# Three cross attentions over 1,500 keys: more probabilities turned by VectorE, moves issued from two queues, router logits made transposed

## The reference, cut to what matters

```
keys   = values = rope(ctx)                      # 1500 x 64, the same in all three layers
scores = q @ keys.T                              # (56 tokens x 16 heads) x 1500
probs  = softmax(scores, axis=-1)
out    = (probs @ values) @ folded_output
```

```
dom    = softmax(gelu(mean_tokens(h) @ te_W1 + b1) @ te_W2 + b2) @ affinity.T    # one row per sequence
logits = h @ Wr.T + dom[sequence]                # 896 tokens x 64
```

## Time and profile before

| | us |
|---|---|
| median of 3 runs | 3226.8 (3226.05 to 3234.65) |
| profiled execution, its own time | 3225.33 |
| its span | 3223.5 |
| TensorE busy | 2964.8 (92%) |
| VectorE busy | 1783.4 (55%) |
| ScalarE busy | 1324.0 (41%) |
| POOL busy | 808.5 (25%) |

### The profile page before, as it was taken

The page is one execution under the profiler, slowest core; times in us unless marked ns, Lnnn a source line. Parts: engine busy times, 40 slices in busy tenths (PEclk is TensorE's granted clock), DMA queues, the critical chain, the costliest instruction groups (busy, mean ns, idle before and its releaser), DMA issues. The chain is left out here.

```text
span 3223.5 us, 49820 instructions
## 1 busy us (share of the span) xinstructions
PE 2964.8 (92%) x18697; PEld 1751.9 (54%) x18697; DVE 1783.4 (55%) x3608; ACT 1324.0 (41%) x2300; POOL 808.5 (25%) x743
## 2 busy tenths in 40 slices
PE   4889999978999989899999989989899999677999
PEld 3755555564455453355655657753355566446444
DVE  6567777723232257777775233347777775655222
ACT  4456666611111142466665122222466665424221
POOL 4324444400316024322232000004322332201000
PEclk8899999978999999999999999999999999888999
DMA  1245556412122202255654010012255564001111
GB/s 32 68 121 142 129 146 140 120 50 97 61 92 78 88 26 82 57 136 131 135 136 124 30 41 26 26 39 78 56 133 133 134 138 121 15 12 23 40 39 33
DMA packets 221451, 266.71 MB, mean 83 GB/s; under 512 B 127178, under 2 KB 148796, under 8 KB 218764
## 3 DMA queue, kind: packets, MB, share of 16 engines
q1 hardware_dynamic: 220348, 262.19, 31.5%
q10 hardware_dynamic: 864, 1.33, 0.1%
HBM read 120.92 MB, written 21.38 MB: 44 GB/s over the span
## 5 line engine op out<-in xcount | busy, mean ns | idle before, releaser
L1777 ACT ACTIVATE l2x_shared<-l2x_shared,l2x_a_low 128x1500 f32<-128x1500 f32 x112 | 173.2, 1546 | 140.8 <-DVE l2x_shared L1733 136.8
L1777 ACT ACTIVATE l1x_shared<-l1x_shared,l1x_a_low 128x1500 f32<-128x1500 f32 x112 | 173.3, 1547 | 138.9 <-DVE l1x_shared L1733 134.9
L1777 ACT ACTIVATE l0x_shared<-l0x_shared,l0x_a_low 128x1500 f32<-128x1500 f32 x112 | 173.4, 1548 | 125.0 <-DVE l0x_shared L1733 122.4
L1647 PE MATMUL l2x_a_S_ps<-l2x_kt,l2x_a_q 64*128 64x366 f32 (+1 forms) x896 | 171.9, 501 | 1.7 <-DMA l2x_a_q<-l2x_qa 1.1
L1647 PE MATMUL l0x_a_S_ps<-l0x_kt,l0x_a_q 64*128 64x366 f32 (+1 forms) x896 | 172.0, 501 | 0.5 <-DVE l0x_shared L1733 0.5
L1647 PE MATMUL l1x_a_S_ps<-l1x_kt,l1x_a_q 64*128 64x366 f32 (+1 forms) x896 | 172.0, 501 | 0.6 <-DVE l1x_shared L1733 0.6
L2016 DVE TENSOR_TENSOR l0f_times_up<-l0f_gate,l0f_U 128x448 f32<-128x448 f32 x64 | 39.8, 622 | 237.3 <-PE l0f_U L1934 237.3
L1985 ACT ACTIVATE l0f_gate<-l0f_G 128x448 f32<-128x448 f32 x72 | 39.2, 544 | 311.1 <-PE l0f_G L1929 311.1
L1733 DVE TENSOR_SCALAR_CACHE_REDUCE l0x_shared<-l0x_a_S_ps 128x768 f32<-128x768 f32 x112 | 107.3, 958 | 102.8 <-PE l0x_a_S_ps L1647 101.8
L1733 DVE TENSOR_SCALAR_CACHE_REDUCE l2x_shared<-l2x_a_S_ps 128x768 f32<-128x768 f32 x112 | 107.3, 958 | 85.2 <-PE l2x_a_S_ps L1647 83.3
L1733 DVE TENSOR_SCALAR_CACHE_REDUCE l1x_shared<-l1x_a_S_ps 128x768 f32<-128x768 f32 x112 | 107.3, 958 | 84.9 <-PE l1x_a_S_ps L1647 82.8
(11 more groups left out here) (667 smaller groups left out, 6623.7 us busy)
## 6 DMA issues: line engine op xcount, KB each, us to landing
l0x_space<-normed SPq DMA_DIRECT2D x192, 96.0 KB
l1x_space<-normed SPq DMA_DIRECT2D x192, 96.0 KB
l2x_space<-normed SPq DMA_DIRECT2D x192, 96.0 KB
l0x_space<-l0x_a_blocks SPq DMA_DIRECT2D x186, 72.0 KB, 2.5
l1x_space<-l1x_a_blocks SPq DMA_DIRECT2D x186, 72.0 KB, 2.3
l2x_space<-l2x_a_blocks SPq DMA_DIRECT2D x186, 72.0 KB, 2.6
l0f_gu<-in_L_ffn_gu SPq DMA_DIRECT2D x36, 256.0 KB, 2.6
l0x_a_q<-l0x_qa SPq DMA_DIRECT2D x32, 224.0 KB, 3.9
```

The costliest lines, as they stand in the source:

```text
L1647: last = pe.matmul(S_ps[:, 2 * pair + rows_, 0:w], q[lane, b % 2, k * 128:(k + 1) * 128], kt[lane, b % 2, pair * W1:pair * W1 + w], start= ...
L1777: act.activation(p[:, n % 2], p[:, n % 2], ACT.Exp, bias=low[:, n % 2, 1:2], scale=-1.0, accum_out=den[:, b % 2, k:k + 1]).then_inc(exp_re ...
```

## The change

Of the 1,500 keys, VectorE now turns 1,024 (NB = 8 slots of 128) and TensorE 476 (NP = 4 slots of 119).

- `turn` does four transposes of 119, into one half of T_ps (T_ps[n % 2]), and so waits for the copy of tile n - 2. `keep` is one copy of 512.
- `block_turn` turns 1,024 columns. Moved rows of group 0 are 4 KB instead of 3 KB, those of group 1 are 3 KB instead of 2.25 KB; POOL's own copies grow alike.
- `values`: slots 0 to 3 come from `pt`, 4 to 11 from the moved blocks. Group 0 is split 2, 2, 4, 4 over its tiles instead of 3, 3, 3, 3.
- `move`: SP issues the DMAs of two lanes (6 of 12) for each group; ScalarE's queue issues the other 6, at tiles 3 and 6, behind exp(n + 2).
- The reciprocals are taken once a batch.
- The columns of the scores are laid out anew, so that TensorE's and VectorE's parts are each in one piece; for it the turned keys of stage 0 are copied by four copies instead of two.
- The rope tables hold each value once, and POOL's three multiplications read them through a view that gives each value twice.
- Router: the token part of the logits is made transposed (64 experts x 512 tokens, two chunks each), the first half ahead of the small network, the second inside it; `dom` is added to both, ScalarE and VectorE copy one half each, and eight transposes bring them to lg_ps.

The diff, cut to its core:

```diff
-KD, KP, KJ = 128, 122, 6
+KD, KP, NB, NP = 128, 119, 8, 4
+NS = NB + NP
...
+        def times(out, src, table):
+            n = src.shape[2] // 2
+            return pool.tensor_tensor(out.rearrange("p s (f two) -> p s f two", two=2), src.rearrange("p s (f two) -> p s f two", two=2),
+                                      table.unsqueeze(3).to_broadcast([KD, NS, n, 2]), ALU.mult)
...
-    W1, W2, JB = 3 * KD, 3 * KP, KJ * 32
-    PIECES = {5: (0, 0, 3), 6: (0, 3, 6), 7: (0, 6, 9), 8: (0, 9, 12), 9: (1, 0, 4), 10: (1, 4, 8), 11: (1, 8, 12)}
+    W1, W2, JB = 3 * KD, KD + 2 * KP, NB * 32
+    PIECES = {5: (0, 0, 2), 6: (0, 2, 4), 7: (0, 4, 8), 8: (0, 8, 12), 9: (1, 0, 4), 10: (1, 4, 8), 11: (1, 8, 12)}
...
-                    move(sp, b, 0, range(4))
+                    move(sp, b, 0, range(2))
...
-                    move(sp, b, 1, range(4) if b + 1 < B else range(2))
+                    move(sp, b, 1, range(2))
...
-                    if ctx is not None and n % T == 5 and n // T + 1 < B:
-                        pe.wait_ge(k_kept, 2 * (n // T + 1) + 2)
-                    for g in range(2):
-                        if n > 0:
-                            pe.wait_ge(pt_kept, 2 * (n - 1) + g + 1)
-                        for k in range(3):
...
-                        last.then_inc(turned, 1)
+                    if ctx is not None and n % T in (5, 6) and n // T + 1 < B:
+                        pe.wait_ge(k_kept, 4 * (n // T + 1) + (1, 4)[n % 2])
+                    if n > 1:
+                        pe.wait_ge(pt_kept, n - 1)
+                    for k in range(NP):
+                        at = TURNED_AT[k]
+                        last = pe.transpose(T_ps[0:KP, n % 2, k * 128:(k + 1) * 128], p[:, n % 2, at:at + KP], m.ident[:])
+                    last.then_inc(turned, 1)
...
                     dve.transpose(blocks[g][:, :, k - FIRST[g]].rearrange("q l j b -> q j l b"),
-                                  p[:, n % 2, 0:2 * W1].rearrange("q (j l b) -> q j l b", j=KJ, l=4)).then_inc(blocked, 1)
+                                  p[:, n % 2, 2 * KP:LK - 2 * KP].rearrange("q (j l b) -> q j l b", j=NB, l=4)).then_inc(blocked, 1)
...
                     block_turn(n)
-                    invert(n)
+                    if n % T == T - 1:
+                        invert(n // T)
...
-                    for g in range(2):
-                        act.wait_ge(turned, 2 * n + g + 1)
-                        act.copy(pt[:, 3 * g:3 * g + 3, :, k * 64:(k + 1) * 64],
-                                 T_ps[0:KP, g, 0:W1].rearrange("k (j o q) -> k j o q", j=3, o=2)).then_inc(pt_kept, 1)
+                    act.wait_ge(turned, n + 1)
+                    act.copy(pt[:, :, :, k * 64:(k + 1) * 64],
+                             T_ps[0:KP, n % 2, :].rearrange("k (j o q) -> k j o q", j=NP, o=2)).then_inc(pt_kept, 1)
...
                     act.copy(kt[:, b % 2, 0:W1], T_ps[:, 0, 0:W1]).then_inc(k_kept, 1)
-                    act.copy(kt[:, b % 2, W1:W1 + W2], T_ps[:, 1, 0:W2]).then_inc(k_kept, 1)
+                    act.copy(kt[CW:128, b % 2, W1:W1 + W2], T_ps[CW:128, 1, 0:W2]).then_inc(k_kept, 1)
+                    act.copy(kt[0:CW, b % 2, W1:W1 + 2 * KP], T_ps[0:CW, 1, KD:W2]).then_inc(k_kept, 1)
+                    act.copy(kt[0:CW, b % 2, W1 + 2 * KP:W1 + W2], T_ps[0:CW, 1, 0:KD]).then_inc(k_kept, 1)
...
                     if n + 2 < N:
                         exp(n + 2)
-                move(act, B - 1, 1, range(2, 4))
+                    if k in (3, 6):
+                        move(act, b, k // 6, range(2, 4))
...
+                def logits(g):
+                    for c in range(DC):
+                        pe.matmul(lgt_ps[g][:], wr[:, c, :], m.ht[:, c, g * 512:(g + 1) * 512], start=(c == 0), stop=False)
+
+                logits(0)
...
+                logits(1)
                 pe.wait_ge(td_done, 1)
...
                 pe.wait_ge(dom_ready, 1)
+                for g in range(2):
+                    pe.matmul(lgt_ps[g][:], dom[:], own[:, g * 512:(g + 1) * 512], start=False, stop=True).then_inc(lgt_made, 1)
                 for t in range(NT):
-                    for c in range(DC):
-                        pe.matmul(lg_ps[:, t, :], m.ht[:, c, t * 128:(t + 1) * 128], wr[:, c, :], start=(c == 0), stop=False)
-                    last = pe.matmul(lg_ps[:, t, :], own[:, t * 128:(t + 1) * 128], dom[:], start=False, stop=True)
+                    if t % 4 == 0:
+                        pe.wait_ge((lgt_act, lgt_dve)[t // 4], 1)
+                    last = pe.transpose(lg_ps[:, t, :], lgt[:, t * 128:(t + 1) * 128], m.ident[0:E, 0:E])
```

More of the change, by code:

```diff
@@ L1624, in turn_keys @@
                     if b > 0:
-                        pe.wait_ge(pt_kept, 2 * n + 2)
-                    for i in range(KJ):
-                        k = KD if i < 3 else KP
-                        last = pe.transpose(T_ps[:, i // 3, i % 3 * k:(i % 3 + 1) * k],
+                        pe.wait_ge(pt_kept, n + 1)
+                    for i in range(NS // 2):
+                        k = KD if i < 4 else KP
+                        at = i % 3 * KD if i < 4 else KD + (i - 4) * KP
+                        last = pe.transpose(T_ps[:, i // 3, at:at + k],
                                             v[0:k, b % 3, 2 * i:2 * i + 2].rearrange("p a e -> p (a e)"), m.ident[0:k, 0:k])
@@ L1680, in values @@
                             out = C_ps[odd * CW:(odd + 1) * CW, g, 0:z - a]
-                            if j < KJ:
-                                last = pe.matmul(out, v[0:KP, b % nv, KJ + j, :], pt[:, j, odd, a:z], start=(j == 0), stop=False)
-                            else:
-                                r, i = (j - KJ) // 3, (j - KJ) % 3
-                                last = pe.matmul(out, v[:, b % nv, 2 * i + r, :],
-                                                 moved_to[g][:, 2 * odd:2 * odd + 2, :, j - KJ, :].rearrange("k q t b -> k t q b"),
-                                                 start=False, stop=(j == 2 * KJ - 1))
-                        if j == KJ - 1:
+                            if j < NP:
+                                last = pe.matmul(out, v[0:KP, b % nv, SLOTS[j], :], pt[:, j, odd, a:z], start=(j == 0), stop=False)
+                            else:
+                                last = pe.matmul(out, v[:, b % nv, SLOTS[j], :],
+                                                 moved_to[g][:, 2 * odd:2 * odd + 2, :, j - NP, :].rearrange("k q t b -> k t q b"),
+                                                 start=False, stop=(j == NS - 1))
+                        if j == NP - 1:
                             last.then_inc(pt_used, 1)
-                    if end < 2 * KJ:
+                    if end < NS:
                         return
                     if b + 1 == B:
-                        pe.wait_ge(rden_ready, after)
+                        pe.wait_ge(rden_ready, B)
                         for t in range(COUNT[g]):
@@ L1732, in negate @@
                             dve.wait_ge(passed, 2 * n + 1)
-                        dve.tensor_scalar(p[:, n % 2, at:at + 2 * w].rearrange("q (a k) -> q a k", a=2),
+                        start = n % 2 * LK + at
+                        dve.tensor_scalar(ahead.shared[:, start:start + 2 * apart].rearrange("q (a k) -> q a k", a=2)[:, :, 0:w],
                                           S_ps[:, 2 * pair:2 * pair + 2, 0:w],
@@ L2140, in l0_router @@
         mx = st.sb("r_mx", [128, NT])
+        lgt = st.sb("r_lgt", [E, NTOK])
         h1_ps = st.ps("r_h1_ps", [128, 512])
+        dom_ps = h1_ps[0:B, 256:512]
         td_ps = st.ps("r_td_ps", [B, 512])
         tdt_ps = st.ps("r_tdt_ps", [B, 512])
-        dom_ps = st.ps("r_dom_ps", [B, 512])
+        lgt_ps = [st.ps(f"r_lgt_ps{g}", [E, 512]) for g in range(2)]
         lg_ps = st.ps("r_lg_ps", [128, NT, E])
+        lgt_made = st.sem("r_lgt_made")
+        lgt_act = st.sem("r_lgt_act")
+        lgt_dve = st.sem("r_lgt_dve")
         ct_ps = [st.ps(f"r_ct_ps{g}", [96, NTOK], BF16) for g in range(2)]
@@ L2196, in _ @@
                 act.activation(td[:], td[:], ACT.Exp).then_inc(td_exp, 1)
+                act.wait_ge(lgt_made, 1)
+                act.copy(lgt[:, 0:512], lgt_ps[0][:]).then_inc(lgt_act, 1)
                 act.wait_ge(shifted, 1)
```

79 lines of the change are left out of this document (40 added, 39 removed).

## The result

The changed kernel is slightly slower. The median of 20 runs is 3238.8 us (3231.32 to 3249.74), against 3230.95 (3220.6 to 3241.19) for 20 runs of the kernel before beside them: ratio 1.0025, 95% interval [1.0015, 1.0035], some 8 us. That is within the 9.7 us that the prediction called no change, 42 us from its forecast and just above its range.

What follows compares the result with a forecast made beforehand. TensorE's order of turn, scores and values was taken as the bound. Terms -13 - 13 + 9 - 7 - 5 = -29 us took the profiled 3,225.3 to 3,196, so a median of 3,197 us; range 3,157 to 3,234.

Steps and rivals of the forecast that it cites:

- Stage 0: Cross attention of stage 0: the turn of the keys takes 1.56 of the 1.53 us saved; +9 us in all.
- late issues: DMA issues on ScalarE's queue are not always quick; charged 0.6 us per batch, bounds 0 and 1.5.
- The four key copies: Copies of the turned keys in stage 0: four take 1.2 us where two took 0.84.
- The saving per tile: TensorE's turn with four transposes instead of six: 0.22 us less per tile, 1.53 per batch, leaving 24.47.
- Late exp in stages 1 and 2: TensorE waiting for exp behind ScalarE's issues: 0.1 us for the tight fit plus 0.6 for slow issues, per batch.
- VectorE and POOL: VectorE's larger transpose fits its idle time; POOL's larger copies and its rotation through the new view add nothing.
- the rival with the strided price: POOL's rotation in stage 0 costs as the strided row, +2.4 us, and bounds the batch: +21, 3,218 us; chance 0.13.
- ends: Ends of the stages: inverses and last moves come sooner, about -2.3 us per stage, -7 in all, bounds 0 and -12.
- The router: Token logits made earlier, partly inside the small network, instead of 13.4 us at half clock: -5 us.
- the other case: Router: -8 us if the earlier matmuls bring the clock to its full level.
- The slower rival, longer issues: ScalarE's six issues in mid-loop take over 4.13 us, deciding from 4.8; at 5.3 us the kernel takes 3,265; chance 0.20.
- the rival with free issues: ScalarE's issues hide under exp and cost nothing: stages 1 and 2 give 24 us each, 3,163 in all; chance 0.17.

Runs made afterwards that it cites:

- SP alone: Changed kernel with SP issuing all twelve moves of each group: in stage 0 only, 3194.7 us; in all three stages, 3227.08 us.
- the threes: Changed kernel with ScalarE's six issues cut into threes, at k = 3 and 4 and at k = 6 and 0, in every stage: 3179.94 us.

## Why the prediction was wrong

**The step that failed** is the one headed "Stage 0". It put the turn of the keys at 3.4 us against 1.84, with 0.6 for late issues, and took the clock as 1.00 throughout. The mechanism was right: the copy of tile 4 is queued behind six issues. Its wait was sized about right too, 1.5 + 0.6 = 2.1 us a batch against 32.2 / 14 = 2.3. But nothing was charged for what TensorE's idle time does to the clock: 19.6 us in the loop, seen as 4.66 us for tile 5 and taken away by matmuls whose results nothing reads. The four key copies cost what the text gave them: with SP alone the keys take 5.53 - 3.54 against 1.84 and tile 5 takes 3.29 against 3.10, 0.34 us together, forecast 0.36. The step's own total did not hold that, though: 3.4 less 1.84 is 1.56, of which 1.5 is the wait and 0.06 is left for the copies, 4 us too little over the loop. The loop got 39.3 us longer and 9 were forecast; clock 20, copies 4, wait 2 and the smaller saving of the next paragraph 5 make 31, where 30 lie between the two.

**The saving per tile** was the second miss. A turn of four spaces the scores 0.63 us behind its start (473.94 to 474.57), not 0.59, so 0.17 us a tile are saved and not 0.22; an undisturbed batch is 24.76, not 24.47. Over 48 batches this is 14 us, 5 of them in stage 0.

**Late exp in stages 1 and 2**: 0.1 + 0.6 was charged; batches average 0.31 and 0.53 over 24.76. A stage's first batch is short when nothing delays it (22.5 and 22.9 us with the threes, 25.8 and 26.1 here), and with that counted the late exp and the half clock behind it cost 0.5 and 0.7. Together with the miss before it, -11.0 and -8.9 us over 15 batches stand where the sum had -12.5: nearly right, in part by errors of opposite sign.

**Right**: VectorE and POOL cost nothing; the rope was no slower, so the rival with the strided price falls; ends -8.2 (forecast -7); issues ran beside the exp, six of group 0 in 4.33 us on average in stage 1 (forecast 4.1 to 4.5), 4.62 in stage 0. **The router** gave 9.4 in this pair of profiles and 7 in others, not 5: the first half of the logits keeps TensorE busy and the second runs at full clock, near the -8 that the text named as the other case.

**The sum again** with measured terms: -13 and -7 for stages 1 and 2, +34.5, -9.4, -1.2 for the projection, -0.9 and -3.9 between, +6.7 ahead of stage 0 by chance: +5.7, and the profiled times differ by 6.0. The slower rival, longer issues, was not the cause: the series of group 0 in stage 0 averaged 4.62 us, under the 4.8 from which it decides, though four of 16 took 5.6 us and more. No rival had the clock in it. Two slips changed no reading: exp of tile 6 is put at 7.8, ahead of the end at 7.9 of the copy that it stands behind, and the rival with free issues takes 14 for ends and router where the sum has 12.

## What to carry to other kernels

A compute engine can issue DMAs beside its running instruction, but what outlasts that instruction delays the next one: cut a series so that each part ends with its cover (here three issues for an exp of 1.55 us), and look for the one place where the delayed copy has no buffer behind it. When a step adds idle time to TensorE, add a term for the clock behind it, unless the row shows the clock holds; here it was 20 us beside waits of 32. Two edits that only make sense together (the second bank and the moved issues) must be priced together: one alone cost 131 us.

## What the runs showed of the hardware

- Behind 2.6 to 3.8 us of TensorE's idle time (in two parts, around 0.83 us of work; more in the first batch) the clock fell from 2.4 to 1.2 GHz in 11 of the 15 batches of stage 0 that turn keys, mostly for 3.4 us. In the four others it held, though TensorE was idle for 3.1 us in the same two parts. With 1.6 us of matmuls in the first part, and 0.6 to 1.6 us idle left behind the keys, it stayed at 2.4 in nearly all.
- ScalarE's exp took 1.55 us with or without six issues beside it. The copy behind it was late by what outlasted the exp: idle 2.44 us behind six issues, 0.73 behind three.
- Moves of one size (96 KB) landed at very different times behind their issue: with SP alone in stage 1, one series 1.6 us and another 7.6 us behind its last issue.
- A multiplication on POOL whose table of half the size repeats each value through a view took 907 ns for 384 columns, where the table read in full took 1.00 us.
